# A mixture-of-experts stage in half tiles: a new order of accumulate, gather and low part on GpSimd

## What the reference computes

```python
probs = jax.nn.softmax(xf @ router_w.T, axis=-1)
topv, topi = jax.lax.top_k(probs, 2)
mask = jnp.zeros_like(probs).at[jnp.arange(n)[:, None], topi].set(1.0)
probs = probs * mask
probs = probs / (probs.sum(axis=-1, keepdims=True) + 1e-09)
g = jnp.einsum('nd,edf->nef', xf, gate_w) + gate_b
u = jnp.einsum('nd,edf->nef', xf, up_w) + up_b
h = jax.nn.silu(g) * u
expert_out = jnp.einsum('nef,efd->ned', h, down_w) + down_b
y = jnp.einsum('ne,ned->nd', probs, expert_out)
x = _layernorm(x + y)
```

## Time and profile before

| | us |
|---|---|
| median of 3 executions | 1410.28 (1407.58 to 1411.42) |
| profiled execution, its own time | 1410.19 |
| span in its trace, first to last instruction | 1408.3 |
| experts, first transposes of rows to last accumulate | 998.0 to 1375.8 |
| half tiles, first matmul of tile 16 to last accumulate | 1280.6 to 1375.8 |

### The profile page before, as it was taken

The page is one execution under the profiler, slowest core; times in us unless marked ns, Lnnn a source line. Parts: engine busy times, 40 slices in busy tenths (PEclk is TensorE's granted clock), DMA queues, the critical chain, the costliest instruction groups (busy, mean ns, idle before and its releaser), DMA issues. The chain is left out here.

```text
span 1408.3 us, 30098 instructions
## 1 busy us (share of the span) xinstructions
PE 1275.2 (91%) x10053; PEld 1081.1 (77%) x10053; DVE 833.3 (59%) x1643; ACT 948.4 (67%) x2118; POOL 739.2 (52%) x837
## 2 busy tenths in 40 slices
PE   5999999999999999999899999954599999998780
PEld 5888888888888888888667777734488888888780
DVE  4454554554555554555468888846466666666564
ACT  4777777777777777778646777745466666565553
POOL 1344444444444444444557777720467777776653
PEclk9999999999999999999989999975799999999895
DMA  4332232222222222222133444313356666666737
GB/s 165 91 107 84 77 95 69 85 64 83 77 84 76 77 64 82 84 68 77 62 104 82 117 116 106 90 61 97 120 140 160 156 160 157 156 157 151 183 65 246
DMA packets 155791, 151.30 MB, mean 107 GB/s; under 512 B 48882, under 2 KB 124250, under 8 KB 155674
## 3 DMA queue, kind: packets, MB, share of 16 engines
q1 hardware_dynamic: 140698, 129.18, 30.1%
q0 software_dynamic: 14976, 20.62, 8.1%
HBM read 113.45 MB, written 33.84 MB: 105 GB/s over the span
## 5 line engine op out<-in xcount | busy, mean ns | idle before, releaser
L367 POOL TENSOR_SCALAR_AFFINE_SELECT a_decay<-a_decay 128x256 f32<-128x256 f32 x256 | 110.7, 436 | 265.1 <-ACT a_decay L447 265.1
L568 DVE TENSOR_TENSOR a_probs<-a_ps_s,a_decay 128x384 f32<-128x384 f32 x256 | 135.0, 553 | 112.6 <-PE a_ps_o L735 73.6
L561 DVE SCALAR_TENSOR_TENSOR a_qk<-a_qk_exp,a_qk_relu 128x512 f32<-128x512 f32 x128 | 91.4, 714 | 151.9 <-ACT a_qk_relu L421 151.9
L1853 POOL DMA_INDIRECT sum_rows<-e_y_out,e_target x78 | 125.8, 1613 | 81.5 <-ACT e_y_out L1907 54.2
L376 POOL TENSOR_TENSOR a_key_sum<-a_probs 128x256 f32<-128x256 f32 x128 | 97.5, 761 | 110.4 <-DVE a_probs L568 110.4
L420 ACT ACTIVATE a_qk_exp<-a_ps_qk 128x512 f32<-128x512 f32 x124 | 74.2, 599 | 109.5 <-PE a_ps_qk L663 108.9
L663 PE MATMUL a_ps_qk<-a_xT_hi,a_w_hi 128*128 128x256 f32 x496 | 139.0, 280 | 1.1 <-DVE a_xT_lo L536 1.1
L663 PE MATMUL a_ps_qk<-a_xT_lo,a_w_hi 128*128 128x256 f32 x496 | 138.5, 279 | 0.0
L663 PE MATMUL a_ps_qk<-a_xT_hi,a_w_lo 128*128 128x256 f32 x496 | 138.4, 279 | 0.0
L445 ACT ACTIVATE a_decay<-a_c_rows,a_c_col 128x256 f32<-128x256 f32 x256 | 129.5, 506 | 0.0
L1834 POOL DMA_INDIRECT e_x_in<-x_rows,e_index x78 | 80.7, 1035 | 79.6 <-DVE e_index L1999 57.0
(11 more groups left out here) (306 smaller groups left out, 3899.8 us busy)
## 6 DMA issues: line engine op xcount, KB each, us to landing
a_c_rows<-a_c_scratch SPq DMA_DIRECT2D x128, 256.0 KB, 3.2
e_gu_raw<-in_L_ffn_gate_w SPq DMA_DIRECT2D x23, 512.0 KB
e_gu_raw<-in_L_ffn_up_w SPq DMA_DIRECT2D x23, 512.0 KB
e_dn_raw<-in_L_ffn_down_w SPq DMA_DIRECT2D x23, 512.0 KB
a_x_in<-in_x SPq DMA_DIRECT2D x16, 256.0 KB
a_x_res<-in_x SPq DMA_DIRECT2D x16, 256.0 KB, 2.8
x_rows<-a_x SPq DMA_DIRECT2D x16, 256.0 KB, 3.3
x_bo_rows<-a_x_bo SPq DMA_DIRECT2D x16, 256.0 KB, 3.9
```

The source lines that it names most:

```text
L367: pool.affine_select(out=d, in_=d, compare_op=ALU.is_ge, fill=0.0, base=0, pattern=[[0, 2], [1, P]], channel_multiplier=-1)\
L561: vec.scalar_tensor_tensor(qk[g][:], qk_exp[g % 2][:], 1.0, qk_relu[g % 2][:], ALU.min, ALU.add).then_inc(qk_done, 1)
L568: vec.tensor_tensor(probs[:, h, :], ps_s[h][:, 0:TRI], decay[h][:], ALU.mult)\
L1853: pool.indirect_dma_start(sum_dram, bass.IndirectOffsetOnAxis(target[par][:, blk:blk + 1], 0), y_out[par][:, blk, :], None, compute_op=ALU ...
```

## The change

Only POOL's order in the half tiles changes; no instruction is added or removed, and the large tiles stay as they are. In tile 16, the first half tile, POOL now makes the low part of tile 17, then issues the gathers of tile 18, and then the four accumulates of tile 15, which is the last large tile. In tiles 17 to 21 it issues the accumulates of t - 1, then the gathers of t + 2 (as far as there is such a tile, that is in tiles 17 to 20), and makes the low part of t + 1 last.

```diff
             def tile(t, par, turn):
-                if has(t, 1):
+                half_phase = isinstance(t, int) and t >= BIGS
+                if has(t, 1) and (not half_phase or t == BIGS):
                     low_parts(1 - par, turn + par)
+                if half_phase and t == BIGS and has(t, 2):
+                    gather_rows(t + 2, par, turn + 1)
                 if has(t, -1):
                     add_rows(t - 1, 1 - par, turn - 1 + par)
-                if has(t, 2):
+                if has(t, 2) and not (half_phase and t == BIGS):
                     gather_rows(t + 2, par, turn + 1)
+                if has(t, 1) and half_phase and t > BIGS:
+                    low_parts(1 - par, turn + par)
```

## The result

The changed kernel takes 1446.99 us (median of 4, 1445.36 to 1448.78) against 1408.93 us for the kernel before (4 runs, with the three shown above). The ratio is 1.0267, with a 95% interval of 1.0255 to 1.0280: 38 us slower. The forecast was 1448.7 us. The profiled execution of the changed kernel took 1445.36 us, with a span of 1443.6 us.

The account below looks back on a forecast made before the run. PE bounds the kernel (91% busy), but in the half tiles POOL's queue would gate each tile start. 8.9 + 23.3 + 5.0 + 1.3 = 38.5 us more gives about 1448.7 us, range 1441 to 1457 (chance 0.66).

Parts of the forecast that it names:

- Part one: Tile 16: earlier gathers shrink PE's 6.29 us wait to some 0.3 us; the accumulates of tile 15 end 4.5 us later.
- part two: Tile 17: POOL's accumulates, gathers and low part run late, so tile 18 starts at 1319.9, not 1310.97: +8.9 us.
- the landing: Tile 17: 6.5 us from the last accumulate of tile 15 to the first of 16; lower bound 4.7 us.
- Part three: Tiles 18 to 20: each takes 18.94 us with 1.3 us of clock loss, together +23.3 us.
- the loop: Tiles 18 to 20: start, 8.10 us to POOL's accumulates, 9.34 us to the low part's end, 0.2 us to next start: 17.64 us.
- Part four: Tile 21, without gathers: 15.6 us to the start of tile 22 in place of 10.56, +5.0 us.
- The end: Tile 22: no low part and its order unchanged, it only starts at the lower clock: +1.3 us.
- The order's aim: Rival, half tiles: the waits for rows and two clock losses go, 13.9 us less, 1396.3 us; chance 0.03.
- a clock that stays low: Rival, half tiles: with PE idle nearly half of each tile the clock stays low, 1458 to 1467 us; chance 0.13.

Follow-up runs that it names:

- tile 16's order alone: Kernel before with the new POOL order in tile 16 only, tiles 17 to 21 as before: ratio 1.0006, no change.
- filler: Changed kernel with transposes of a constant in PE's idle time at the end of tiles 17 to 21: ratio 1.0203 against the kernel before.
- low part ahead of the gathers: Changed kernel with POOL's low part before the gathers in tiles 17 to 20, still behind the accumulates: ratio 1.0179 against the kernel before.
- low part off POOL: Changed kernel with the low parts of tiles 18 to 22 made by DVE, accumulates still before gathers: ratio 1.0024 against the kernel before.
- late low part alone: Kernel before with the new order (accumulates, gathers, low part) in tiles 17 to 21 only, tile 16 as before: ratio 1.0258.
- with the gathers first: Kernel before with half tiles ordered gathers, low part, accumulates on POOL, and DVE writing the index at the tile's start: ratio 0.9973.
- the last kernel: Kernel before with gathers before accumulates in half tiles, late index, low parts of tiles 18 to 22 on DVE: ratio 0.9924.

## Why the prediction was right, and where its terms were off

The sum was made from S(17) on, and I compare it from there: 114.3 us from S(17) to the end of the span before (1408.3 - 1294.00), 153.7 us after (1443.6 - 1289.88), which is 39.4 us more, against a sum of 38.5. The stages up to S(17) were 4.1 us shorter in this execution; the change does not touch them, and the medians differ by 38.1 us.

- **Part one, the gathers of tile 18.** Right. They leave at 1290.07, 0.2 us after S(17) (forecast 0.04 us), and PE waits for no rows of tile 18. The wait that was to take its place was put at some 16 us and is 13.91 us; part two says why. The accumulates of 15 were put at 7.21 us; beside the rest they took 8.27 us (1292.74 to 1301.01).
- **Part two, tile 17: +8.9 forecast, +6.3 measured** (23.22 - 16.97). The mechanism is right, the landing was mis-sized. From the last accumulate of 15 to the first of 16 it takes 3.48 us (1301.01 to 1304.49) and not 6.5. The gathers in between leave at 1.0 us each, which takes off 0.8 us, and the accumulates of 15 end 11.1 us after S(17), not 9.8, which adds 1.3 us. With the same order in tile 16, four other runs show 3.2 to 4.1 us (3.4 tile 16's order alone, 3.2 filler, 4.1 low part ahead of the gathers, 3.9 low part off POOL). The late low part alone, whose tile 16 has the order of before, shows 7.8 us. A row each of the changed kernel and of that run (columns as in the earlier trace rows):

```profile
1294.00:1302.00 8.00, 5.19 (x44) 4.98 (x42) 6.74 (x18) 5.98 (x13) 6.09 (x4) 1.00 1.06 261
...
1296.00:1304.00 8.00, 3.04 (x26) 2.83 (x24) 3.30 (x7) 3.03 (x7) 4.58 (x4) 0.88 1.04 266
```

The DMA share is near 1.0 until 1302 in the one and until 1304 in the other, and the landing is seen some 2.5 us after that in both, at 1304.49 and 1306.42. So the price went with how long the transfers stay busy, and not with the place in the program, by which I chose 6.5; no run moved the transfers by themselves, so this is not shown as the cause. The 6.5 us was also no landing that the trace names: the accumulate at 1305.76 has [0.80 <-issue], behind the low part.

- **Part three, tiles 18 to 20: +23.3 forecast, +25.2 measured** (58.71 - 33.55). Without the clock the loop was put at 17.64 us; the filler run shows 17.57 to 17.59. The clock was put at 1.3 us for a tile. From a start to the next transposes it is 7.35, 7.99, 8.33 and 8.54 us at tiles 18 to 21 in place of 5.85, so 1.5, 2.1, 2.5 and 2.7 us. I had taken the loss from the two long waits before, after which the lower level ended within some 3 us. Here it lasts 5 us and more from tile 19 on, as the windows above show. The length of the wait does not set this: after 8.20 us the late low part alone loses 1.3 us at tile 21 (7.13 us), and after 4.9 us the low part ahead of the gathers loses 2.6, 2.7 and 1.3 us at tiles 19 to 21 (8.44, 8.53 and 7.12 us). What does, these runs do not say. POOL's accumulates begin 9.6, 10.3 and 10.6 us after S(18), S(19) and S(20), forecast 9.4, later by this clock term alone.
- **Part four: +5.0 forecast, +7.2 measured** at S(22), of which 1.4 us is the clock. The other 0.9 us is a gap that I misread. The accumulates of 20 begin at 1383.49, 1.76 us after ACT's scaling ended, where tiles 18 to 20 have 0.9 us; before, it is 1.76 us too (ending at 1353.48), and so it is in the late low part alone, the filler run and the low part ahead of the gathers. I had read that start as the landing of tile 19's accumulates, at 6.9 us. In the changed kernel those were issued by 1365.89, 17.6 us before, and the gap is the same, so it was never the landing. What it is, stays open. The end: +1.3 forecast, +0.8 measured.
- **The rivals.** The order's aim, no wait for rows, was reached in full, and it was worth 11.9 us of PE's waits; it could not show, since 44.3 us of another wait came in. The case of a clock that stays low was half right in kind: it lasts longer than in the trace before, and costs some 9 us net by the filler run and not 6.5. The landing and the gathers, too dear by 3.8 us together, made up for most of that and of the gap at tile 21. So the total is nearer than its terms, and that nearness is luck: the mechanism was right, the errors of size cancelled.

The loop itself is shown four times: by taking it alone (36 us), by leaving it out (0 us), by shortening it by the gathers (12 us) and by taking the low part out of it (34 us).

## What to carry to other kernels

In an in-order queue, what another engine needs at the start of the next tile must not stand behind work whose input comes late in this one; count the queue from the latest input, here 8.1 us, and compare the end of the chain with the consumer's next start. Two operations that wait on the same queue can't be judged by moving one: the gathers came earlier and the low part paid almost four times as much (44.3 us of waits for 11.9). Where PE idles before every tile, add its clock to each round, and measure it at the place where the round starts.

## What the runs showed of the hardware

- A DVE instruction can be held for the whole length of a POOL elementwise instruction. A cast of 128x2 took 3.46 us beside POOL's 128x512 pair and 0.16 us without it; a subtraction of 128x1024 took 2.65, 2.81 and 4.67 us in place of 1.22 us (in the kernel before, with the gathers first, and at 1385.92 in tile 21 of the changed kernel, beside the low part at 1386.45), and each time it ended 1.1 us after POOL's low part. The Trainium skill says in "GPSIMD Engine Reference", section "Key points", that GpSimd shares its SBUF interfaces with VectorE, so that it contends with VectorE's instructions in a two-port mode or with two SBUF inputs. The subtractions have two inputs in SBUF, and for them the traces agree; whether the cast ran in a two-port mode, no row shows. That section gives no size; here the size was a whole pair of POOL instructions for two columns of work.
- After a wait, the lower clock level lasted between 2.8 and 6.3 us with PE fully busy (read from the pace of its matmuls, 0.21 us at the lower level and 0.12 us at the upper), and the length of the wait did not order these times: 3.0 us after a wait of 6.3 us (before, tile 17), 3.5 us after 13.9 us and 5.0 to 6.3 us after 8.2 us (changed kernel), but 2.9 us after 8.20 us (late low part alone, tile 21) and 5.9, 6.1 and 2.9 us after 4.9 us (low part ahead of the gathers). After waits of 1.04 us and less before the starts of the last kernel it did not show. Filler transposes of a constant kept the level at 1.00 and gave back 9 us net, without any change to the work.
- The four accumulates of tile 15 landed between 3.2 and 7.8 us after the last was issued, in the runs whose trace shows POOL waiting for them; in the longest case the DMA engines were busy at a share near 1.0 until 2.4 us before the landing was seen, and weight loads (issued from 1294.96) and gathers (from 1298.92) ran in that stretch.
